# One decoder layer over 16 sequence positions: turn ahead of scores and values, second row chain, positions and plan moved

## The reference

```python
# 1: a recurrence over the first axis, then a norm over the rows
k, v, r = ((mu * x + (1 - mu) * x_prev) @ W.T for each of k, v, r)
# numerator and denominator: decayed sums of exp(k) * v and exp(k) over the steps before, and the current one by exp(u)
x = layernorm(x + sigmoid(r) * numerator / denominator @ W_out.T)
# 2: cross attention to the context, 16 heads of 16
attn = softmax(clip(q @ k.T * scale, -CLAMP, CLAMP))
x = layernorm(x + (attn @ v) @ Wo + bo)
# 3: mixture of 16 experts: sigmoid gate, 2 of 4 groups, 4 experts a row, and 2 shared ones
combine = top-4 weights, normalised
routed = einsum("tef,ehf,te->th", silu(x @ w1) * (x @ w3), w2, combine)
x = layernorm(x + routed + shared)
```

## Time and profile before

| | us |
|---|---|
| median of 3 runs | 1068.57 (1068.05 to 1074.94) |
| profiled execution | 1061.99 |
| its span, first to last instruction | 1060.2 |
| TensorE busy | 968.2 (91%) |
| VectorE busy | 772.2 (73%) |
| ScalarE busy | 687.2 (65%) |
| GpSimd busy | 594.0 (56%) |
| mean granted clock of TensorE, share of full | 0.98 |

### The profile page before, as it was taken

How to read it: one execution, slowest core, us unless ns; L and a number is a source line. 1 busy time by engine, 2 the same in 40 slices (tenths; PEclk the granted TensorE clock), 3 DMA queues, 4 the chain that set the end, 5 groups by cost and what they waited for, 6 DMA issues and landing times.

```text
span 1060.2 us, 21641 instructions
## 1 busy us (share of the span) xinstructions
PE 968.2 (91%) x6502; PEld 750.1 (71%) x6502; DVE 772.2 (73%) x1666; ACT 687.2 (65%) x2182; POOL 594.0 (56%) x651
## 2 busy tenths in 40 slices
PE   4678999999999999989999999888799999999896
PEld 2456667777777677667776776667688888887775
DVE  3477999999999999999999999763432222465687
ACT  1168777767868777766777777774446556666533
POOL 4552464766756746747467473222545555666654
PEclk8789999999999999998999999999999999999998
DMA  9804334433343331113111110113345544788765
GB/s 256 247 19 147 97 118 160 133 127 130 131 162 129 117 121 60 49 53 119 47 60 50 60 43 28 63 58 106 125 121 155 153 143 123 247 258 259 233 216 182
DMA packets 97872, 135.38 MB, mean 128 GB/s; under 512 B 11203, under 2 KB 83554, under 8 KB 97761
## 3 DMA queue, kind: packets, MB, share of 16 engines
q1 hardware_dynamic: 84704, 101.53, 31.7%
q0 software_dynamic: 13056, 32.47, 8.3%
HBM read 61.91 MB, written 76.23 MB: 130 GB/s over the span
## 4 chain that ended last, share of the span: by engine, by line
PE 64%; DVE 13%; POOL 8%; issue 8%; ACT 4%; another core or an unknown queue 1%; DMA 1%; SPq 1%; DVEq 0%; POOLq 0%; ACTq 0%
PE bU L580 8%; PE bT L594 7%; PE four L849 6%; PE four L775 6%; PE four L890 5%; PE bT L849 5%; PE bM L713 5%; DVE Sc L1337 4%; PE bO L811 4%; POOL mix L1673 3%; PE bM L580 3%; PE bM L740 3%; POOL mix L1671 2%; DVE wkv L1314 2%; POOL rstd L1653 1%
## 5 line engine op out<-in xcount | busy, mean ns | idle before, releaser
L1070 ACT ACTIVATE Sc<-Sc,nmx 128x256 f32<-128x256 f32 x512 | 253.6, 500 | 5.1 <-DVE nmx L1339 5.1
L1078 ACT ACTIVATE PT<-bT 128x512 f32<-128x512 f32 x256 | 151.7, 593 | 142.4 <-PE bT L594 141.0
L1733 POOL DMA_INDIRECT Yt<-PT,dests x150 | 150.1, 1001 | 108.9 <-issue 56.4
L1337 DVE TENSOR_SCALAR Sc<-four 128x1024 f32<-128x1024 f32 x128 | 156.1, 1220 | 36.3 <-PE four L775 29.7
L594 PE MATMUL bT<-idn,Sc 128*128 128x128 f32 x1024 | 163.4, 283 | 6.6 <-ACT PT L1078 5.6
L594 PEld LDWEIGHTS bT<-idn,Sc 128*128 128x128 f32 x1024 | 115.6, 142 | 73.2 <-issue 60.6
L1339 DVE TENSOR_REDUCE nmx<-Sc 128x4 f32<-128x1024 f32 x128 | 156.2, 1220 | 4.4
L1716 POOL DMA_INDIRECT Xs<-x,slots x120 | 120.1, 1001 | 35.2 <-issue 18.6
L1070 ACT ACTIVATION_READ_ACCUMULATOR Sc<-Sc,nmx 128x1 f32 x512 | 99.0, 193 | 0.0
L775 PE MATMUL four<-KT,QT 32*128 32x256 f32 x1024 | 76.3, 408 | 12.8 <-DVE Sc L1337 9.0
L1449 DVE SCALAR_TENSOR_TENSOR tgb<-tgb,four 128x256 f32<-128x256 f32 x47 | 19.7, 420 | 90.4 <-ACT tgb L1123 85.1
(11 more groups left out here) (229 smaller groups left out, 2004.6 us busy)
## 6 DMA issues: line engine op xcount, KB each, us to landing
Xs<-yg SPq DMA_DIRECT2D x16, 1768.0 KB, 8.2
xb<-Xs SPq DMA_DIRECT2D x152, 136.0 KB
yg<-Yt SPq DMA_DIRECT2D x27, 512.0 KB
W<-w SPq DMA_DIRECT2D x4, 1152.0 KB, 11.3
xTs<-xT SPq DMA_DIRECT2D x16, 256.0 KB
x<-x SPq DMA_DIRECT2D x16, 256.0 KB
Base<-stg SPq DMA_DIRECT2D x15, 256.0 KB
out<-acc SPq DMA_DIRECT2D x15, 256.0 KB
```

The source lines that it names most:

```text
L1070: last = fn(Sc[:, n % 3, m, t, :], Sc[:, n % 3, m, t, :], ACT.Exp, bias=nmx[:, n % 3, m, t:t + 1], accum_out=rs[:, s % 2, t, h:h + 1])
L1078: fn(flat(PT[:, h % RING]), bT[:, :], ACT.Copy).then_inc(a_pt.sem, 1)
L1337: ts(Sc[:, n % 3].rearrange("p m t k -> p (m t k)"), flat(score_banks(n)), CLAMP, -CLAMP, ALU.min, ALU.max).then_inc(d_clip.sem, 1)
L1733: pool.indirect_dma_start(Yt, bass.IndirectOffsetOnAxis(ap=dests[:, i % IDS, b:b + 1], axis=0), y_rows(i)[:, b, :], None, bounds_check=SPA ...
```

## The change

No instruction is added or taken away; the order is changed on each engine.
- TensorE: in each slot the first turn comes first, then the scores, and right behind them the values (they stood behind the slot's other work). `t_chunk` 2 stands ahead of the turn in g2, `t_chunk` 5 behind the second turn in g5, and in g7 the shared expert's last product (`t_chunk` 8) ahead of the positions (`t_chunk` 7).
- VectorE: in g2 the sum and moments of x2 ahead of the clip; in g7 `shared_sum` ahead of `router(t, 2)`. The plan's parts ahead of the recurrence's work of g0, and part 1 in slot 4 where it was in slot 1.
- ScalarE: in g0 the copy of the turned reciprocals (rT) ahead of that of the attention output (ao).
- GpSimd: the two roots (`roots`) between the second and the third mix; they stood behind the third.

```diff
-PLAN_AT = {0: 0, 1: 1, 7: 2}
+PLAN_AT = {0: 0, 4: 1, 7: 2}
...
@@ TensorE, slot
+                if A and g == 3:
+                    context_k(a, 0)
+                if T and g == 2:
+                    t_chunk(t, 2)
+                if heads:
+                    turn_probs(n, 0)
                 if 0 <= n + 2 < PAIRS:
                     scores(n + 2)
-                if A and g == 3:
-                    context_k(a, 0)
-                if heads:
-                    turn_probs(n, 0)
+                if g % 2 == 0 and 0 <= n - 2 < PAIRS:
+                    values(n // 2 - 1)
                 if A and g == 5:
                     project_q(a)
                 if s in PLANS and g == 0:
                     count(PLANS[s])
...
+                if T and g == 0:
+                    t_chunk(t, 0)
                 if T and g == 1:
                     t_chunk(t, 1)
-                if T and g == 2:
-                    t_chunk(t, 2)
...
-                if T and g == 5:
-                    t_chunk(t, 5)
...
-                if g % 2 == 0 and 0 <= n - 2 < PAIRS:
-                    values(n // 2 - 1)
-                if T and g == 0:
-                    t_chunk(t, 0)
                 if heads:
                     turn_probs(n, 1)
...
+                if T and g == 5:
+                    t_chunk(t, 5)
                 if T and g == 6:
                     t_chunk(t, 6)
                 if T and g == 7:
+                    t_chunk(t, 8)
                     t_chunk(t, 7)
-                    t_chunk(t, 8)
@@ VectorE, slot
+                if T and g == 2:
+                    t_chunk(t, 2)
+                    dve.wait_ge(d_z2.sem, d_z2.at(t))
+                    moments(1, t, x2[:, t % 2, :, 0:D])
...
                 if 0 <= n + 2 < PAIRS:
                     clip(n + 2)
+                if s in PLANS and g in PLAN_AT:
+                    plan(PLANS[s], PLAN_AT[g])
                 if A and g == 0:
                     invert(a, 1)
                     finish_wkv(a)
...
                 if T and g == 7:
+                    shared_sum(t)
                     router(t, 2)
-                    shared_sum(t)
@@ GpSimd, step (first_mixes holds the waits and dx)
                 if B:
-                    mixes(b)
+                    mixes(b, 0)
                 pairs(1)
                 pairs(2)
-                if A:
-                    rsqrt(0, a)
-                if T:
-                    rsqrt(1, t)
+                roots(s)
+                if B:
+                    mixes(b, 1)
                 send(s - 2, 1)
```

More of the change, by code:

```diff
@@ L1581, in slot @@
                     fold_bv()
-                if s in PLANS and g in PLAN_AT:
-                    plan(PLANS[s], PLAN_AT[g])
                 if T and g == 1:
                     t_chunk(t, 1)
-                if T and g == 2:
-                    t_chunk(t, 2)
-                    dve.wait_ge(d_z2.sem, d_z2.at(t))
-                    moments(1, t, x2[:, t % 2, :, 0:D])
                 if A and g == 2:
@@ L1656, in final_rsqrt, with mixes @@
                 rsqrt(2 + l % 4, l // 4)
-            def mixes(s):
-                pool.wait_ge(s_xT[s % 2], 16 * (s // 2 + 1))
+            def mixes(s, part):
                 now, before = xTs[:, s % 2], xTs[:, 1 - s % 2]
-                if s:
-                    pool.wait_ge(p_kvr.sem, p_kvr.at(s - 1))
-                    pool.wait_ge(d_wkv.sem, d_wkv.at(s - 1))
-                pool.tensor_tensor(dx, now, before, ALU.subtract).then_inc(g_dx.sem, 1)
-                pool.wait_ge(g_dx.sem, g_dx.at(s))
-                for m in range(3):
+                if part == 0:
+                    first_mixes(s, now, before)
+                for m in (2,) if part else (0, 1):
                     mu = vec[:, m, :].rearrange("p (j a) -> p j a", a=1).to_broadcast([P, ND, TOK])
@@ L1673, in mixes, with first_mixes, roots @@
                     pool.tensor_tensor(mix[:, m], mix[:, m], before, ALU.add).then_inc(g_mix.sem, 1)
+            def first_mixes(s, now, before):
+                pool.wait_ge(s_xT[s % 2], 16 * (s // 2 + 1))
+                if s:
+                    pool.wait_ge(p_kvr.sem, p_kvr.at(s - 1))
+                    pool.wait_ge(d_wkv.sem, d_wkv.at(s - 1))
+                pool.tensor_tensor(dx, now, before, ALU.subtract).then_inc(g_dx.sem, 1)
+                pool.wait_ge(g_dx.sem, g_dx.at(s))
+            def roots(s):
+                if 0 <= s + 1 < L:
+                    rsqrt(0, s + 1)
+                if 0 <= s - 1 < L:
+                    rsqrt(1, s - 1)
             def sum_num(s):
```

## The result

The changed kernel takes 1078.64 us (median of 14 runs, 1072.83 to 1083.44), the kernel before 1065.96 us (14 runs). The ratio is 1.0112, 95% interval 1.0089 to 1.0136: 1.1% slower. The medians differ by 12.7 us; the prediction's sum was +13.7. It said 1082 us because it started from 1068.6, the median of three runs, which is 2.6 us over that of fourteen. The profiled execution took 1072.8 us with a span of 1071.0, which is 10.8 us over the span of before. It is the fastest of the 14 runs and has the highest mean granted clock, 0.984; the other thirteen have 0.974 to 0.983, and the five over 1081 us have 0.974 to 0.979. So a typical run has more time at half clock than this profile, and where in the kernel is not known.

The account below looks back on a forecast made before the run. TensorE (91% busy) and VectorE (73%) were taken as nearly full, so waits inside a step count. Twelve steps +12.7, steps 0 and 14 +1.6, plan -0.6: +13.7 on 1068.6, 1082 us; 8-in-10 range 1063 to 1091.

Parts of the forecast that it names:

- The pair: Scores directly ahead of values on TensorE: saves 0.15 us for each even slot, bounds nothing and 0.26.
- Piece A: Plain step from VectorE's clip of g0 to the scores of g4, 17.56 us before: longer by 0.92.
- Piece B: Plain step from the scores of g4 to those of g6, 10.64 us before: longer by 0.48.
- Piece C: Plain step from the scores of g6 to the next clip of g0, 13.21 us before: shorter by 0.34.
- The sum: Whole plain step, the three pieces together: +1.06 us, from 41.41 to 42.47.
- row chain: Sum, moments, root and norm of x2 come earlier: priced at nothing, worth up to 0.15 us without piece A's hold.
- steps 0 and 14: Main loop steps with both copies but less other work: +0.8 us each, between 0 and 1.06.
- The plan: Step 10: half of the 3.4 us of lost clock gained, -1.7; with the step's +1.06, -0.6.
- Steps 9 and 11 to 13: Counted among the twelve plain steps, each forecast to be longer by 1.06 us.
- The total: Whole kernel: +13.7 us, giving 1082 us.
- Rival 4: TensorE's new waits in g2, g4 and g6 let the clock fall: +14 us more, 1096; chance 0.08.

Follow-up runs that it names:

- e10: Changed kernel with GpSimd's third mix ahead of the roots again from step 1 on; 1079.13 us.
- e2: Changed kernel with ScalarE's copy of K in g3 moved behind the slot's second copy of probabilities; 1067.65 us.
- e1: Changed kernel with TensorE's scores ahead of the first turn again in even slots, values and t_chunk 0 at their old place; 1082.73 us.
- e4: Kernel before with only GpSimd's two roots moved ahead of the third mix; 1102.45 us.
- e3: Changed kernel with t_chunk 2 back behind scores and turns on TensorE and behind the clip on VectorE; 1104.41 us.
- e6: Kernel before with the plan's parts moved as in the change and roots ahead of the third mix in steps -2 to 0 only; 1058.84 us.
- e12: Changed kernel with ScalarE's copies of K and of the queries both behind their slot's second copy of probabilities; 1065.99 us, ratio 1.0018 to the kernel before.
- e9: Kernel before with the plan's parts moved and roots early in steps -2 to 0 only, timed with an interval; 1060.12 us, ratio 0.9943 to the kernel before.
- e5: Kernel before with GpSimd's roots ahead of the third mix and the step's two sends between roots and mix; 1090.82 us.
- e7: Kernel before with TensorE's values directly behind the scores and the first turn behind both; 1104.41 us.
- e8: Changed kernel with GpSimd's sends between the roots and the third mix; 1102.69 us.

## Why the prediction was right or wrong

**The pair.** Right: 1.08 from scores to values, which saves the 0.15. The Trainium skill, page "TensorEngine Tiling (Array Packing)", section "Tiling Modes", says that each change of the tiling mode drains TensorE, and so counts a third one between scores and values. The trace does not contradict it: scores take 1.08 in front of values and 1.08 in front of a plain turn.

**Piece A, +0.92.** Measured +1.04 (18.60 against 17.56). The waits are those it named: 0.78 in front of the output projection where it said about 1, and in g4 0.49 for ScalarE's PT where it said 0.9. The other 0.41 stands one turn earlier, as a wait for x2, which it had put ahead of the copy; with that wait taken away the one for PT is 0.89 (e10). e2 gives the copy of K's share, 0.57; e10 shows that the copy and not x2 ends last there.

**Piece B, +0.48.** Right to the hundredth: 11.12. The turn of g6 waits 0.44 where it said 0.5. e1 brings 10.64 back by the order on TensorE alone. **Piece C, -0.34.** Measured -0.38; TensorE's wait in front of the positions is gone. The sum, +1.06, was measured as +1.14.

**"I price it at nothing" (row chain), and no price for the roots.** Right only for the two together, and only in a plain step: 42.55 with the roots on either side of the third mix (after, e10). Alone the early roots cost about 3 us a step (e4), since the norms then meet the third mix, and in most steps the half clock comes behind it. The row chain moved forward is what keeps the change out of that: taken back, it costs 2.1 to 4.0 us a step (e3). The prediction gave the chain a worth of "up to 0.15". The step of the prediction that failed is that it judged GpSimd's move by what waits for GpSimd, and did not ask which VectorE instruction would then run beside which mix.

**Steps 0 and -1.** "I take 0.8 each" for steps 0 and 14. Step 0 became 0.6 shorter (38.9 against 39.5), and the start as a whole gained 4.4 us: VectorE's norms there did wait for the root (3.01 and 1.99 us), and the prediction did not look at these steps. e6 shows this gain without the rest of the change: 3.7.

**The plan.** "I take half, -1.7", -0.6 with the step's own loss. Measured -3.2 with that loss. e6, which has the plan's move without the new order, gives its worth alone: -3.7, over the upper bound of 3.4. That bound was only the clock that was lost; 0.93 became 1.00, and of the wait of 3.39 a part went as well. Taking half was a guess on the low side.

**Steps 9 and 11 to 13.** Missed: +1.64 a step in 11 to 13 where +1.06 was given, and step 9 (43.11) is like them. In step 12 of after VectorE's clip starts 1.73 us after the scores of g6 (plain step: 1.22), and TensorE then waits for the hidden product behind it. TensorE, VectorE, GpSimd:

```profile
595.07 1.15 PE L775 MATMUL four<-KT,QT 32*128 32x256 f32 x16
...
600.11 1.99 PE L713 MATMUL bM<-ao,W 128*128 128x256 f32 x8 [0.54 <-DVE stg L1440]
```

```profile
596.80 1.23 DVE L1337 TENSOR_SCALAR Sc<-four 128x1024 f32<-128x1024 f32 x1 [2.67 <-PE four L775]
```

```profile
596.07 0.97 POOL L1726 DMA_INDIRECT Xs<-x,slots  x1 [0.30 <-issue]
```

GpSimd issues an indirect DMA just there, 1.0 us behind the scores; in steps 3 and 4 it comes some 4 us later. That this is the cause is not shown. In step 8 one stands 1.07 us behind the scores and the clip starts on time (1.21), and no run took the DMA away. This stays open.

**Step 14.** +3.2 where +0.8 was given. A is longer by 1.26, B by 0.52, C by 1.38. The clock makes C longer: e10 has the same step up to the scores of g6, to the hundredth, and the same wait of 1.79 us for VectorE's hidden product in front of the shared expert. There the clock stays full and the step takes 41.16, in after the product behind the wait takes 3.13 instead of 1.99. After, then e10, and the windows of both steps:

```profile
685.15 3.13 PE L713 MATMUL bM<-ao,W 128*128 128x256 f32 x8 [1.79 <-DVE stg L1440]
```

```profile
689.99 1.99 PE L713 MATMUL bM<-ao,W 128*128 128x256 f32 x8 [1.79 <-DVE stg L1440]
```

```profile
651.53:694.26 42.73, 36.67 (x286) 26.98 (x286) 36.03 (x74) 30.04 (x98) 11.67 (x18) 0.96 0.09 33
```

```profile
656.37:697.53 41.16, 35.10 (x286) 25.98 (x284) 35.85 (x73) 30.00 (x98) 11.65 (x17) 1.00 0.09 34
```

So 1.6 of the 3.2 us are the half clock and 1.6 the order. It is not bound to the place of the third mix: of the orders with this clock in step 14, after, e2 and e12 have it behind the roots, e6 and e9 in front.

**The total.** +13.7 forecast, +10.8 measured in the profile. The forecast per plain step was good to 0.08 us; two gains (together 7.6 us, where the prediction had 0.6 for the plan and a loss at the start) and losses in steps 11 to 14 (some 4 us beyond the forecast) lay outside it and partly cancelled. So the mechanism of the plain step was right, and that the total came so near is in part luck. The prediction took everything up to 1079 us as no change that a measurement tells; with 14 runs on either side the interval shows the 1.1% clearly. Rival 4, the half clock, did not occur in a plain step of the profiled execution, but it did in step 14, and the lower mean clock of the other thirteen runs says that they had more of it. In the plain steps of e1, e3, e4, e5, e7 and e8 it mostly came behind a wait of over 1.1 us for x2. In step 12 of e1, step 3 of e5 and step 11 of e9 it came 6 to 7 us behind the clip of g0, where TensorE's longest wait in the step so far had been 0.55, 0.91 and 0.71 us.

## What to carry to other kernels

Putting an instruction behind a wait is priced by what stands ahead of the releaser on the releaser's own engine: here two long copies on ScalarE, and moving them gave back 0.75 of the 1.14 us of a step (0.57 for the copy of K, 0.18 for that of the queries). Before moving such an instruction back, look for what waits for itself: the scores of g6 then waited for the copy of the queries. When an elementwise instruction on GpSimd is moved, list the VectorE instructions that read and write SBUF alone in the stretch it moves to, and compare their lengths, not their idle time, before and after. Cut a change of several moves by stretch of the run: here the two that gained (e9, 0.9943) were worth having without the rest.

## What the runs showed of the hardware

- VectorE's norms (128x256, SBUF to SBUF) take 0.73 us a pair beside GpSimd's small work and 2.46 beside its 128x512 products; a 128x2 instruction (L1253) takes 0.17 or up to 1.26. In the fourteen traces together (before, after, e1 to e12) these two instructions take over 0.15 us more than alone 301 times, and each time they end 0.02 to 0.17 us after an instruction of GpSimd. The clip and the maximum (L1337, L1339; 1.22 each) kept their length beside the same mixes: none of them takes over 1.23 in any trace.
- Whether that happens can hang on 0.25 us of phase. It can strike GpSimd's old order too: in step 11 of e9 a stretch at half clock made L1253 start 1.4 us later, beside a mix; it took 1.05, and the step 43.80. And a wait of TensorE for x2 of 1.1 to 2.9 us was in some steps, not in all, followed by a stretch at 0.50 of the clock: in e8 the same wait of 2.27 stands in steps of 43.82 at the full clock and in steps of 45.2 and more with that stretch.
- Of the twelve runs with the early first root, after among them, eleven had the clip of g0 of step 1 at 88.4 to 92.4 us. e10 had it at 96.23, although its order up to there is that of after; before and e7, without the early root, had 95.65 and 95.21. Step 15 and the tail, the same in all, took 376.8 to 387.4 us, in ten of the fourteen profiled executions under 380.6. So the gain of after's start, 4.4 us, is one draw from a spread of several us, and single totals can't judge parts of the change.
